# A graph network kernel: taking edges behind sixteen tiles, and loading and turning weights behind the first tiles

## The chip, the cores and the metric

One core of a Trainium2 chip runs the whole program. The metric is the device time of one execution in microseconds, as the median of several runs.

## The reference

Two layers of a graph network on x of 50000 x 256, with one edge list of 75000 edges (12500 random pairs both ways and one loop per node), sorted by target:

```python
h = relu(layernorm(x))
x = x + gcn(h)                # first layer
h = relu(layernorm(x))
x = x + attention(h, src, dst)  # second layer
# gcn: t = h @ w1.T + b1; t = relu(batchnorm(t)); t = (t @ w2.T + b2) @ w_gcn.T
#      degrees by target, norm = dinv[src] * dinv[dst], segment_sum of t[src] * norm
# attention: q, k, v of 8 heads; softmax over the edges of a row; sum of v; @ Wo + bo
```

The batch norm needs the mean and variance of `h @ w1.T + b1` over all rows, so the first matmul must be finished for all rows before the second one starts.

## The kernel before

The program is a row of stages, each a block in which the engines run side by side and meet through semaphores. The change is in the first two.

The rows of x come in 98 tiles of 512 (128 partitions with 4 rows each). **The first stage** (the block that begins at L463, 0 to 607 us) does this for tile t: SP loads x (L499); DVE takes row statistics (L215, four instructions, and L219); ACT takes the root (`a_std`, L648); DVE forms reciprocal and shift (L226, L228); ACT writes the normalised rows `a_hn` (L652, four instructions); PE turns them into `a_turn_ps` (L680); ACT copies that to `a_ht` (L642); PE multiplies by the turned w1 into `a_h_ps`, called `h1_ps` in the code (L702); ACT copies it to `h` with the bias (L634) and stores it (L627); DVE takes its statistics for the batch norm (L1024). Each engine's program is a sequence of steps, and a step holds work of several tiles, in a fixed order: in step s ACT stores tile s-5, copies out `h` of s-4, copies `a_ht` of s-2 and then does root and `a_hn` of tile s; PE turns tile s-1 and multiplies tile s-3; DVE does statistics, one-hots and scale of tile s, then the batch norm statistics of tile s-5, then what is written beside tile s. x, `a_hn`, `a_ht` and `h` have two buffers each, `h1_ps` has one.

Beside the tiles the stage prepares the edges. At tile 1 DVE packs an edge into a word (`pack_words`, L780), at tile 3 it closes the words (`close_words`, L800) and then takes the edges that are no loops out of the 588 columns (`take_all`, L843): a take is a MAX8 on each half of the words and a MATCH_REPLACE8 on each, and moves 16 columns into `found`. The number of takes is read from the data. Tiles 4 to 15 carry twelve steps of class work on the 240 columns found (`beside_tile`, L975, counted from `plan.class_tile` = 4). From `plan.hist_pair` = 8 on, that is tiles 16 to 95, six columns per pair of tiles are counted: DVE makes two one-hots a column (L758, L759), PE multiplies them into `hist_ps` (L672), and POOL scatters the column's words into `dst_slots` (L591), three per tile, each group waiting for `a_hn` of a tile and each scatter for the one three before it. `over_pairs` writes the head of the tiles out and runs the others in a hardware loop.

Ahead of its steps ACT issues seven weight loads (L606 to L610), waits for PE to turn w1 and w_gcn (L731) and copies both (L614), waits for PE's product of w2 and w_gcn and of b2 and w_gcn (L736, L739) and copies these (L616, L617), and issues eight loads of Wo (L621). PE does its part of this ahead of its steps as well, through `turn_ps`.

**The second stage** (the block at L1134, 607 to about 1160 us) closes the batch norm (L1287 on), loads `h` again (L1149), applies the norm (`hb`, L1198), multiplies by the mixed weight (`mix_ps`, L1231), adds the bias (L1310) and stores two scaled copies (L1192, L1161); beside it edges are sorted by source in bodies of six tiles, and the projection weights of the second layer are prepared (`find_peak`, L1321, and `split_weights`, L1326). SP first loads `h` of tiles 0 and 1, stores and loads the small tables (L1168, L1169), then loads the projection weights (L1171 to L1173), and then runs its steps, in which it loads h1 of tile s and stores `agg_table` of tile s-4.

Of the kernel before, what the change touches and what calls it, by code (L numbers as in the profile page):

```python
# [34 lines left out]
P = 128  # L35
D = 256
# [23 lines left out]
class Plan:  # L60


    def __init__(self, n, e):
# [167 lines left out]
def build(nc, x, src, dst, w1, b1, gamma, beta, w2, b2, w_gcn, b_gcn,  # L231
# [20 lines left out]
    with ExitStack() as ctx:  # L252
# [92 lines left out]
        with ExitStack() as part:  # L345
# [117 lines left out]
            with ExitStack() as inner, nc.Block() as block:  # L463
# [23 lines left out]
                def _(sp):  # L487
                    def step(at):
# [11 lines left out]
                        if isinstance(tile, int) and tile == 1:  # L500
                            load_edges()

# [16 lines left out]
                    sp.wait_ge(edges_loaded, 16 * plan.edge_loads)  # L519

# [77 lines left out]
                def _(act):  # L598
# [13 lines left out]
                    for b, w in enumerate((w1_t, wg_t)):  # L612
                        act.wait_ge(weights_turned, b + 1)
                        nc.scalar.activation(w[:, :, :].rearrange("p a b -> p (a b)"), turn_ps[0][:, b * TILE:(b + 1) * TILE], ACT.Copy).then_inc(weights_copied, 1)  # L614
                    act.wait_ge(mixed, 1)
                    nc.scalar.activation(w_mix[:, :, :].rearrange("p a b -> p (a b)"), turn_ps[1][:, 0:TILE], ACT.Copy).then_inc(weights_copied, 1)  # L616
                    nc.scalar.activation(b_mix[:, :], turn_ps[1][:, TILE:TILE + D], ACT.Copy).then_inc(weights_copied, 1)  # L617
                    rows_of_head = wo.rearrange("(d h) n -> h d n", h=H)
                    for h in range(H):
                        kc, first = divmod(h * DH, P)  # L620
                        act.dma_start(w_out[first:first + DH, kc, :], rows_of_head[h]).then_inc(out_loaded, 16)  # L621

                    def step(at):
# [20 lines left out]
                        if at(0) is not None:  # L644
# [9 lines left out]
                            last.then_inc(hn_ready[u], 1)  # L654

                    over_tiles(act, plan, 5, step)
                    act.wait_ge(out_loaded, 16 * H)
# [4 lines left out]
                def _(pe):  # L662
                    def step(at, k, s):
                        if s == plan.degree_step:
                            count_all()
                        if at(1) is not None:
# [15 lines left out]
                            last.then_inc(turned[u], 1)  # L682
                        if s == plan.class_tile + 6:
                            pe.wait_ge(class_ready, 1)
# [40 lines left out]
                    pe.wait_ge(weights_loaded, 16 * 7)  # L725
                    pe.wait_ge(const_ready, const_of_ident)
                    for b, w in enumerate((w1_n, wg_n)):
                        for kc in range(KC):
                            for oc in range(KC):
                                at = b * TILE + kc * D + oc * P  # L730
                                last = nc.tensor.transpose(turn_ps[0][:, at:at + P], w[:, oc, kc * P:(kc + 1) * P], ident[:, :])  # L731
                        last.then_inc(weights_turned, 1)
                    pe.wait_ge(weights_copied, 2)
                    for kc in range(KC):
                        for jc in range(KC):
                            nc.tensor.matmul(turn_ps[1][:, kc * D:(kc + 1) * D], w2_n[:, jc, kc * P:(kc + 1) * P],  # L736
                                             wg_t[:, jc, :], start=jc == 0, stop=jc == KC - 1)
                    for jc in range(KC):
                        last = nc.tensor.matmul(turn_ps[1][:, TILE:TILE + D], b2_c[:, jc:jc + 1].to_broadcast([P, P]), wg_t[:, jc, :],  # L739
                                                start=jc == 0, stop=jc == KC - 1)  # L740
                    last.then_inc(mixed, 1)
                    pe.wait_ge(weights_copied, 4)
                    over_pairs(pe, plan, 3, step, (hist_loop,))

                @block.vector
                def _(dve):
# [53 lines left out]
                    def close_words():  # L800
# [21 lines left out]
                        link(v.tensor_scalar(rounds_f[:, 3:4], rounds_f[:, 2:3], -float(plan.takes_beside - 1), 1.0, ALU.add, ALU.max))  # L822
# [20 lines left out]
                    def take_all():  # L843
# [4 lines left out]
                        hold(dve, replaced, more * 2 + (2 * plan.takes_beside))  # L848
# [126 lines left out]
                    def beside_tile(tile):  # L975
# [29 lines left out]
                    def step(at, k, s):  # L1005
# [27 lines left out]
                    over_pairs(dve, plan, 5, step, (hist_loop,))  # L1033
# [100 lines left out]
            with ExitStack() as inner, nc.Block() as block:  # L1134
# [12 lines left out]
                def _(sp):  # L1147
                    def load_h1(i, u):
# [1444 lines left out]
```

## Time and profile before

| | us |
|---|---|
| median of 3 runs | 3427.66 (3424.08 to 3429.75) |
| profiled execution | 3436.49 |
| its span, first to last instruction | 3434.7 |

| engine | busy us | share |
|---|---|---|
| PE | 3104.5 | 90% |
| DVE | 2809.3 | 82% |
| ACT | 2502.0 | 73% |
| POOL | 1953.0 | 57% |

The span and the windows are of the one profiled execution. A busy time is the union of an engine's instructions; register work, waits and the issuing of DMAs are not counted. "L215" is line 215 of the kernel. A wait in square brackets is the time that the engine sat idle before an instruction, and what ended it. SPq, ACTq and POOLq are the queues in which an engine issues DMAs. `PEclk` is the granted clock of TensorE as a share of 2.4 GHz; 0.50 is 1.2 GHz.

### The profile page before, as it was taken

To read this page: it belongs to the slowest core of one execution; us is meant where nothing else is said; L and a number is where in the kernel's file an instruction comes from. 1 tells how busy PE (TensorE), PEld (TensorE's weight loads), DVE (VectorE), ACT (ScalarE), POOL (GpSimd) and SP (SyncE) were. 2 spreads that over 40 slices of the span, in tenths; PEclk is the share of its full clock that TensorE was granted. 3 is DMA by queue.
4 is the path that set the end of the run, shared out by engine and by line. 5 is a ranking of instruction groups with operands and counts; after the bars stand their busy time and mean duration, and the time that the engine had idled before them with its cause. 6 is when DMAs were issued, how large, how long until landed. Compare 5 with 4: busy or idle time off the path is not lost. (4 is left out here: it accounts for less than half of the span.)

```text
span 3434.7 us, 80752 instructions
## 1 busy us (share of the span) xinstructions
PE 3104.5 (90%) x20244; PEld 2498.7 (73%) x20244; DVE 2809.3 (82%) x7375; ACT 2502.0 (73%) x7074; POOL 1953.0 (57%) x1668
## 2 busy tenths in 40 slices
PE   2899999799998489999999999994999999999999
PEld 1455554577775278787888878883899999999998
DVE  6888887787886478888888888884888888888887
ACT  2688888699896567676777777762777777777776
POOL 1055554155554377777777777763555555555553
PEclk6899999999999699999999999996999999999999
DMA  2455555688886578888878888865677777777774
GB/s 76 147 204 203 203 202 182 233 300 309 301 306 234 206 271 297 305 296 293 304 293 303 296 305 293 302 257 182 230 249 258 258 254 250 254 254 257 254 248 157
DMA packets 335634, 861.27 MB, mean 251 GB/s; under 512 B 98484, under 2 KB 152923, under 8 KB 323019
## 3 DMA queue, kind: packets, MB, share of 16 engines
q1 hardware_dynamic: 238794, 677.69, 55.3%
q0 software_dynamic: 66256, 78.94, 7.7%
q10 hardware_dynamic: 30512, 103.83, 7.6%
q8 instruction: 27, 0.44, 0.1%
q14 instruction: 45, 0.36, 0.0%
HBM read 521.95 MB, written 416.52 MB: 273 GB/s over the span
## 5 line engine op out<-in xcount | busy, mean ns | idle before, releaser
L1848 PE MATMUL c_qkv_ps<-w_qkv_hi,c_ht_hi 128*128 128x256 f16 x2352 | 642.3, 273 | 0.0
L1848 PE MATMUL c_qkv_ps<-w_qkv_lo,c_ht_hi 128*128 128x256 f16 x2352 | 642.3, 273 | 0.0
L1848 PE MATMUL c_qkv_ps<-w_qkv_hi,c_ht_lo 128*128 128x256 f16 x2352 | 642.3, 273 | 0.0
L2281 ACT ACTIVATE e_mine<-e_mine,e_attention 128x32 f32<-128x32 f32 x2352 | 518.7, 308 | 42.3 <-issue 26.1
L2228 POOL DMA_INDIRECT e_kv<-kv_table,e_near x392 | 401.5, 1024 | 113.4 <-issue 102.7
L1718 POOL DMA_INDIRECT c_got<-y_table,c_near x392 | 395.1, 1008 | 108.7 <-issue 87.9
L591 POOL DMA_INDIRECT dst_slots<-dst_word,dst_goal x240 | 241.3, 1005 | 304.3 <-ACT a_hn L652 235.9
L2317 PE MATMUL e_out_ps<-w_out,e_mean_t 128*128 128x256 f32 x1568 | 392.8, 380 | 0.0
L2220 POOL TENSOR_TENSOR e_kv<-e_kv,e_part_of 128x1024 f32<-128x1024 f32 x98 | 187.0, 1908 | 350.8 <-DVE e_part_of L2550 350.8
L702 PE MATMUL a_h_ps<-a_ht,w_t 128*128 128x512 f32 x784 | 368.9, 614 | 17.8 <-ACT h L634 13.9
L1482 POOL DMA_INDIRECT src_slots<-staged_word,staged_goal x240 | 235.2, 980 | 254.5 <-DVE sort_lane_hot L1371 119.2
L1231 PE MATMUL mix_ps<-w_mix,hb 128*128 128x256 f32 x1568 | 358.0, 382 | 12.7 <-ACT hb L1198 9.8
L1231 PEld LDWEIGHTS mix_ps<-w_mix,hb 128*128 128x128 f32 x1568 | 297.2, 191 | 59.0 <-ACT hb L1198 12.6
L1711 POOL TENSOR_TENSOR c_x<-c_agg,c_x 128x1024 f32<-128x1024 f32 x98 | 231.4, 2361 | 161.3 <-ACT c_agg L1765 151.9
L2317 PEld LDWEIGHTS e_out_ps<-w_out,e_mean_t 128*128 128x128 f32 x1568 | 267.4, 191 | 44.0
L1835 PE MATMUL c_sum_ps<-c_got,c_sum_hot 128*128 128x256 f32 x784 | 217.2, 400 | 87.3 <-DVE c_agg L1957 58.5
L702 PEld LDWEIGHTS a_h_ps<-a_ht,w_t 128*128 128x128 f32 x784 | 144.8, 195 | 184.2 <-issue 184.1
L1776 ACT ACTIVATE c_hn<-c_x,c_shift,c_rstd 128x256 f32<-128x256 f32 x392 | 203.5, 590 | 95.7 <-DVE c_shift L1978 94.8
L1703 POOL TENSOR_TENSOR c_qk<-c_q,c_kv 128x1024 f32<-128x1024 f32 x98 | 232.0, 2367 | 34.9 <-DVE c_kv L1942 32.6
L1848 PEld LDWEIGHTS c_qkv_ps<-w_qkv_lo,c_ht_hi 128*128 128x128 f16 x2352 | 230.5, 98 | 27.1
L1848 PEld LDWEIGHTS c_qkv_ps<-w_qkv_hi,c_ht_lo 128*128 128x128 f16 x2352 | 230.5, 98 | 27.1
L2273 ACT ACTIVATE e_mean_t<-e_mean_ps 128x512 f32<-128x512 f32 x196 | 114.9, 586 | 184.9 <-PE e_mean_ps L2331 163.8
(433 smaller groups left out, 7781.8 us busy)
## 6 DMA issues: line engine op xcount, KB each, us to landing
kv_table<-c_kv SPq DMA_DIRECT2D x98, 1024.0 KB
h_table<-h ACTq DMA_DIRECT2D x98, 512.0 KB
h<-h_table SPq DMA_DIRECT2D x98, 512.0 KB
y_table<-y_out ACTq DMA_DIRECT2D x98, 512.0 KB
agg_table<-agg_out SPq DMA_DIRECT2D x98, 512.0 KB
c_agg<-agg_table SPq DMA_DIRECT2D x98, 512.0 KB
x_table<-c_x SPq DMA_DIRECT2D x98, 512.0 KB
q_table<-c_q SPq DMA_DIRECT2D x98, 512.0 KB
```

The source lines that it names most:

```text
L591: nc.gpsimd.indirect_dma_start(out=dst_slots, out_offset=bass.IndirectOffsetOnAxis(ap=dst_goal[:, k:k + 1], axis=0), in_=dst_word[:, k:k + ...
L702: last = nc.tensor.matmul(h1_ps[:, oc * TILE:(oc + 1) * TILE], w1_t[:, kc, oc * P:(oc + 1) * P], ht[u][:, kc, :], start=kc == 0, stop=kc = ...
L1231: last = nc.tensor.matmul(mix_ps[u][:, j * D:(j + 1) * D], hb[u][:, kc, j * P:(j + 1) * P], w_mix[:, kc, :], start=kc == 0, stop=kc == KC - 1)
L1482: nc.gpsimd.indirect_dma_start(out=src_slots, out_offset=bass.IndirectOffsetOnAxis(ap=staged_goal[h][:, k:k + 1], axis=0), in_=staged_word ...
L1703: nc.gpsimd.tensor_tensor(qk[u][:, :, :], qb[w][:, :, :], kv[w][:, :, 0, :], ALU.mult).then_inc(qk_ready, 1)
L1711: nc.gpsimd.tensor_tensor(x1[u][:, :, :], agg[w][:, :, :], xb[w][:, :, :], ALU.add).then_inc(x1_ready, 1)
L1718: nc.gpsimd.indirect_dma_start(out=got[w][:, j, :], out_offset=None, in_=y_table, in_offset=bass.IndirectOffsetOnAxis(ap=near[w][:, j:j + ...
L1835: last = nc.tensor.matmul(sum_ps[:, j * D:(j + 1) * D], sum_hot[w][:, row, :], got[w][:, row, :], start=True, stop=True)
L1848: last = nc.tensor.matmul(qkv_ps[n][:, j * D:(j + 1) * D], h[u][:, kc, j * P:(j + 1) * P], wt[:, kc, n * D:(n + 1) * D], start=m == 0, sto ...
L2228: nc.gpsimd.indirect_dma_start(out=kv[w][:, j, :], out_offset=None, in_=kv_table, in_offset=bass.IndirectOffsetOnAxis(ap=near[w][:, j:j + ...
L2281: last = nc.scalar.activation(of_head, of_head, ACT.Copy, scale=attention[u][:, j, h, 0:1])
L2317: last = nc.tensor.matmul(out_ps[:, j, :], mean_t[u][:, kc, row * P:(row + 1) * P], w_out[:, kc, :], start=False, stop=kc == KC - 1)
```

## The change

Three parts. First, the weights are turned and mixed within the first steps (PE: turning at step 2, the mix at step 3, its bias at step 5, in `h1_ps` and `hist_ps`; ACT: the copies behind tiles 1, 4 and 5), and the Wo loads go to SP, behind the edge loads. Second, the takes: one behind each of tiles 4 to 19, and a loop of at least one more at tile 20 (`take_rest`). `class_tile` becomes 20 and `hist_pair` 16; the 240 columns are then counted in 30 pairs instead of 40 (`hist_most` 8 instead of 6), so four columns and four scatters a tile. The head, seven pairs with takes, the class tiles and 27 counting pairs alternate between written-out turns and two hardware loops. Third, SP's loads of the projection weights come behind h1 of tile 5, and `find_peak` behind tile 5 instead of tile 3.

```diff
-        self.takes_beside = -(-self.wide // TAKEN)
-        self.most_extra = max(1, self.most_takes - self.takes_beside + 1)
-        self.class_tile = 4
+        self.take_pair = 2
+        self.take_pairs = 8
+        self.takes_beside = 2 * self.take_pairs
+        self.most_extra = max(1, self.most_takes - self.takes_beside)
+        self.class_tile = 2 * (self.take_pair + self.take_pairs)
...
+                take_loop = (3, plan.take_pair + plan.take_pairs)
...
-                    return k is not None or i - plan.hist_pair in hist_pairs
+                    return k == 1 or (k is None and i - plan.hist_pair in hist_pairs)
...  SP, first stage, behind load_edges() at tile 1
+                            for h in range(H):
+                                kc, first = divmod(h * DH, P)
+                                sp.dma_start(w_out[first:first + DH, kc, :], rows_of_head[h]).then_inc(out_loaded, 16)
...  ACT, end of step
+                            if isinstance(i, int) and i * 2 + u == 1:
+                                copy_weights()
+                            if isinstance(i, int) and i * 2 + u == 4:
+                                copy_mix()
+                            if isinstance(i, int) and i * 2 + u == 5:
+                                copy_mix_bias()
...  PE, between turning tile s-1 and multiplying tile s-3
+                        if s == 2:
+                            turn_weights()
+                        if s == 3:
+                            mix_weights()
+                        if s == 5:
+                            mix_bias()
...
-                    over_pairs(pe, plan, 3, step, (hist_loop,))
+                    over_pairs(pe, plan, 3, step, (take_loop, hist_loop))
...  DVE
-                        link(v.tensor_scalar(rounds_f[:, 3:4], rounds_f[:, 2:3], -float(plan.takes_beside - 1), 1.0, ALU.add, ALU.max))
+                        link(v.tensor_scalar(rounds_f[:, 3:4], rounds_f[:, 2:3], -float(plan.takes_beside), 1.0, ALU.add, ALU.max))
...
-                        with dve.Fori(0, more + (plan.takes_beside - 1)) as n:
-                            take(n)
+                        with dve.Fori(0, more) as n:
+                            take(n + plan.takes_beside)
...
                             close_words()
-                            take_all()
+                        elif 0 <= tile - 2 * plan.take_pair < plan.takes_beside:
+                            take(tile - 2 * plan.take_pair)
                         elif at == 0:
+                            take_rest()
                             decode_words()
...
-                            if k is None:
+                            if k == 0:
+                                take(i * 2 + (u - 2 * plan.take_pair))
+                            elif k is None:
                                 beside_tile(i * 2 + u)
...  SP, second stage, in step; the same loads are gone from before over_tiles
+                            if isinstance(i, int) and i * 2 + u == 5:
+                                load_qkv()
...
-                            if isinstance(b, int) and b == 0 and t == 3:
+                            if isinstance(b, int) and b == 0 and t == 5:
                                 find_peak()
```

## Rows read from the trace of the kernel before

**Rows 1.** The page, busy time, share of the span and instructions.

```profile
PE 3104.5 (90%) x20244; PEld 2498.7 (73%) x20244; DVE 2809.3 (82%) x7375; ACT 2502.0 (73%) x7074; POOL 1953.0 (57%) x1668
```

**Rows 2.** Windows: busy us and count by engine, then clock, DMA share, GB/s.

```profile
60.00:80.00 20.00, 0.00 (x0) 0.00 (x0) 19.45 (x89) 0.26 (x1) 0.00 (x0) 0.50 0.00 0
...
120.00:140.00 20.00, 16.53 (x65) 8.63 (x64) 13.37 (x52) 14.01 (x28) 0.00 (x0) 1.00 0.43 157
...
200.00:560.00 360.00, 349.80 (x1317) 185.00 (x1316) 316.67 (x1251) 312.07 (x626) 208.83 (x209) 1.00 0.57 203
```

**Rows 3.** Timeline of the head: start us, duration us, engine, line, operation.

```profile
15.24 3.78 PE L736 MATMUL a_turn_ps<-wg_t,w_n 128*128 128x256 f32 x8 [1.67 <-ACT wg_t L614]
...
24.43 1.28 ACT L648 ACT_TABLE_LOAD   x1 [2.88 <-issue]
...
26.06 0.18 DVE L226 RECIPROCAL a_rstd<-a_std 128x4 f32<-128x4 f32 x1 [19.53 <-ACT a_std L648]
...
36.01 1.40 DVE L215 BATCH_NORM_STATS2 a_stats<-a_x 128x6 f32<-128x256 f32 x4
```

**Rows 4.** The takes: timeline of DVE, and line 836 by itself.

```profile
49.85 0.17 DVE L826 CAST rounds<-rounds_f 128x4 int32<-128x4 f32 x1
...
77.88 1.41 DVE L215 BATCH_NORM_STATS2 a_stats<-a_x 128x6 f32<-128x256 f32 x4 [0.22 <-DVE words L841]
...
L836 DVE MAX8 edge_best<-words x30: 442/452/467, 51.4 to 76.2; 128x8 f32<-128x294 f32 x30
```

**Rows 5.** Timeline of DVE in the class tiles and behind them.

```profile
116.89 0.18 DVE L226 RECIPROCAL a_rstd<-a_std 128x4 f32<-128x4 f32 x1 [0.36 <-ACT a_std L648]
...
123.63 0.18 DVE L226 RECIPROCAL a_rstd<-a_std 128x4 f32<-128x4 f32 x1 [3.44 <-ACT a_std L648]
...
161.84 1.41 DVE L215 BATCH_NORM_STATS2 a_stats<-a_x 128x6 f32<-128x256 f32 x4 [0.21 <-DVE uneven_cols L940]
...
576.57 1.39 DVE L215 BATCH_NORM_STATS2 a_stats<-a_x 128x6 f32<-128x256 f32 x4
```

**Rows 6.** Timeline of ACT at a tile without one-hots.

```profile
582.61 1.27 ACT L634 ACTIVATE h<-a_h_ps,bn_in 128x512 f32<-128x512 f32 x2 [0.17 <-PE a_h_ps L702]
```

**Rows 7.** Timeline of PE: a product among class tiles, columns and product in the loop.

```profile
115.38 5.61 PE L702 MATMUL a_h_ps<-a_ht,w_t 128*128 128x512 f32 x8
...
302.38 0.66 PE L672 MATMUL hist_ps<-hot_hi,hot_lo 128*128 128x392 f16 x3
...
303.99 3.67 PE L702 MATMUL a_h_ps<-a_ht,w_t 128*128 128x512 f32 x8
```

**Rows 8.** Timeline of DVE: one tile of the loop with three columns.

```profile
305.03 0.18 DVE L226 RECIPROCAL a_rstd<-a_std 128x4 f32<-128x4 f32 x1 [0.21 <-issue]
...
308.30 0.38 DVE L219 BATCH_NORM_AGGREGATE a_moments<-a_stats 128x2 f32<-128x6 f32 x4
308.70 0.32 DVE L758 TENSOR_SCALAR hot_hi<-lane,dst_key 128x392 f16<-128x392 f16 x1
...
310.29 0.18 DVE L226 RECIPROCAL a_rstd<-a_std 128x4 f32<-128x4 f32 x1 [0.32 <-ACT a_std L648]
```

**Rows 9.** Timeline of POOL: one of six scatters in a row.

```profile
479.54 0.97 POOL L591 DMA_INDIRECT dst_slots<-dst_word,dst_goal  x1 [0.30 <-issue]
```

**Rows 10.** The second stage: timeline of its start, one window behind it.

```profile
620.00 0.43 SPq L1171 DMA_DIRECT2D w_qkv<-in_L_gnn_Wq  x1
...
630.97 2.93 ACT L1198 ACTIVATE hb<-h,bn_shift,bn_scale 128x512 f32<-128x512 f32 x4 [11.96 <-DMA h<-h_table]
...
632.54 3.72 PE L1231 MATMUL mix_ps<-w_mix,hb 128*128 128x256 f32 x16 [2.39 <-ACT hb L1198]
...
637.50 0.44 SPq L1149 DMA_DIRECT2D h<-h_table  x1
...
641.99 1.52 ACT L1198 ACTIVATE hb<-h,bn_shift,bn_scale 128x512 f32<-128x512 f32 x2 [0.30 <-DMA h<-h_table]
...
700.00:1060.00 360.00, 340.72 (x1672) 262.82 (x1671) 289.74 (x1073) 326.45 (x696) 189.15 (x235) 1.00 0.87 305
```

More of the change, by code:

```diff
@@ L611, in _, with copy_weights, copy_mix, copy_mix_bias @@
                     act.wait_ge(const_ready, const_of_ident)
[L612 to L621, printed above, removed]
+                    def copy_weights():
+                        for b, w in enumerate((w1_t, wg_t)):
+                            act.wait_ge(weights_turned, b + 1)
+                            nc.scalar.activation(w[:, :, :].rearrange("p a b -> p (a b)"), h1_ps[:, b * TILE:(b + 1) * TILE], ACT.Copy).then_inc(weights_copied, 1)
+                    def copy_mix():
+                        act.wait_ge(mixed, 1)
+                        nc.scalar.activation(w_mix[:, :, :].rearrange("p a b -> p (a b)"), hist_ps[:, 0:TILE], ACT.Copy).then_inc(weights_copied, 1)
+                    def copy_mix_bias():
+                        act.wait_ge(mixed, 2)
+                        nc.scalar.activation(b_mix[:, :], hist_ps[:, 0:D], ACT.Copy).then_inc(weights_copied, 1)
                     def step(at):
@@ L723, in count_all @@
                         last.then_inc(all_used, 1)
-                    pe.wait_ge(weights_loaded, 16 * 7)
-                    pe.wait_ge(const_ready, const_of_ident)
[L727 to L740, printed above, removed]
@@ L741, in _, with turn_weights @@
-                    last.then_inc(mixed, 1)
-                    pe.wait_ge(weights_copied, 4)
-                    over_pairs(pe, plan, 3, step, (hist_loop,))
+                    def turn_weights():
+                        pe.wait_ge(weights_loaded, 16 * 7)
+                        for b, w in enumerate((w1_n, wg_n)):
+                            for kc in range(KC):
+                                for oc in range(KC):
+                                    at = b * TILE + kc * D + oc * P
+                                    last = nc.tensor.transpose(h1_ps[:, at:at + P], w[:, oc, kc * P:(kc + 1) * P], ident[:, :])
+                            last.then_inc(weights_turned, 1)
+                        pe.wait_ge(weights_copied, 2)
@@ new lines, in mix_weights, with mix_bias @@
+                    def mix_weights():
+                        for kc in range(KC):
+                            for jc in range(KC):
+                                last = nc.tensor.matmul(hist_ps[:, kc * D:(kc + 1) * D], w2_n[:, jc, kc * P:(kc + 1) * P],
+                                                        wg_t[:, jc, :], start=jc == 0, stop=jc == KC - 1)
+                        last.then_inc(mixed, 1)
+                    def mix_bias():
+                        pe.wait_ge(weights_copied, 3)
+                        for jc in range(KC):
+                            last = nc.tensor.matmul(hist_ps[:, 0:D], b2_c[:, jc:jc + 1].to_broadcast([P, P]), wg_t[:, jc, :],
+                                                    start=jc == 0, stop=jc == KC - 1)
+                        last.then_inc(mixed, 1)
@@ L841, in take, with take_rest @@
                             v.match_replace(out=here, in_to_replace=best[h][:, :], in_values=here, imm_value=NONE).then_inc(replaced, 1)
-                    def take_all():
+                    def take_rest():
                         dve.wait_ge(const_ready, const_all)
                         more = dve.value_load(rounds[0:1, 3:4], min_val=0, max_val=plan.most_extra - 1) + 1
-                        with dve.Fori(0, more + (plan.takes_beside - 1)) as n:
-                            take(n)
-                        hold(dve, replaced, more * 2 + (2 * plan.takes_beside))
+                        with dve.Fori(0, more) as n:
+                            take(n + plan.takes_beside)
+                        hold(dve, replaced, more * 2 + (2 * plan.takes_beside + 2))
                     def decode_words():
@@ L1031, in step @@
                             count_all()
-                    over_pairs(dve, plan, 5, step, (hist_loop,))
+                    over_pairs(dve, plan, 5, step, (take_loop, hist_loop))
                     for u in two:
@@ L1147, in _, with load_qkv @@
                 def _(sp):
+                    def load_qkv():
+                        for i, (w, b) in enumerate(((wq, bq), (wk, bk), (wv, bv))):
+                            sp.dma_start(w_qkv[:, :, i * D:(i + 1) * D], w.rearrange("(c p) n -> p c n", p=P)).then_inc(qkv_loaded, 16)
+                            sp.dma_start(b_raw[:, i * D:(i + 1) * D], b.partition_broadcast(P)).then_inc(qkv_loaded, 16)
+                        sp.dma_start(b_out_n[:, :], bo.partition_broadcast(P)).then_inc(qkv_loaded, 16)
                     def load_h1(i, u):
```

8 lines of the change are left out of this document (3 added, 5 removed).

## The prediction

> **What bounds the kernel now.** The page comes first: PE is busy for 90% of the span [rows 1], so what can be won lies in the stretches where it is not. The windows of that stage show three states: 60 to 80 us with no matmul at all, 120 to 140 us with PE at 16.5 of 20, and 200 to 560 us with 349.8 of 360 [rows 2]. So a whole run of time is lost in the first 160 us, and later the stage runs close to PE's limit. I date everything by VectorE's (DVE's) first instruction of a tile, the row statistics of L215: with tN for tile N, t2 is 36.01, t4 is 77.88, t16 is 161.84 and t96 is 576.57 [rows 3 to 5]. There are four of them in a tile.
>
> Three things hold the head. ScalarE (ACT) copies weights and issues eight loads of the output weight before its first `a_std`, so DVE waits 19.53 us for tile 0 [rows 3]. Behind tile 3 DVE does 30 MAX8 and their replacements in one piece, and PE runs dry [rows 2, 4]. Tiles 4 to 15 carry the class work on DVE: 161.84 - 77.88 = 83.96 us for twelve tiles, with DVE itself waiting at some (3.44 us at tile 10) [rows 5].
>
> From t16 on, 80 tiles take (576.57 - 161.84) / 80 = 5.184 us each. Three limits nearly coincide there. (a) One PSUM buffer: `h1_ps` is filled in 3.67 us [rows 7], then ACT copies it out in 1.27, 0.17 after PE's end [rows 6]: 5.11 us, which I take as the beat of a tile without one-hots, 5.12. (b) PE's own work: 360 / 5.184 = 69.4 tiles with 349.8 busy are 5.04 us each, 0.66 of it three columns, or 0.22 each [rows 2, 7]. (c) DVE: from one reciprocal to the next 310.29 - 305.03 = 5.26, of which 0.32 is waiting, so 4.94; its one-hots run from 308.70 to 309.97, 0.42 a column; all else is 3.67 [rows 8].
>
> **The change part by part**, as DVE's tile dates. The sum is made against the profiled execution, 3436.49 us (span 3434.7 and 1.8 around it), which is 8.8 us above the median of 3427.66; I apply the difference to the median.
>
> *Weights behind the first tiles.* DVE's statistics of tile 0 are done at 26.06 - 19.53 = 6.53. From ACT's table load to the reciprocal it is 26.06 - 24.43 = 1.63 [rows 3], so the reciprocal starts near 8.2 instead of 26.06: -17.9 us. Seven loads stay ahead of it on ACT's queue. The eight loads of `w_out` move to SP's queue, behind the edge loads; SP's next job, x of tile 2, waits for tile 0's `a_hn`, which ends near 10.7 (after the reciprocal as now), and at some 0.4 us an issue the fourteen loads are out by then. Tile 1 then starts 2.7 us later as now, packing starts near 11.2 and t2 is about 18.1 (36.01 - 17.9). The packing needs the edges. The load of x of tile 2 has from 10.7 to 18.1 to land; a load of as many bytes takes 4.5 (637.50 to 641.99) [rows 10].
> The weight work moves into PE's and ACT's queues at tiles 1 to 5. Behind PE's matmuls for the mix at step 3 (3.78 us [rows 3]) and the fewer for its bias at step 5 (half as many) stand the products of tiles 0 and 2, behind these `h` on ACT, and behind `h` the `a_std` of tiles 4 to 6, for which DVE waits. For tile 4: tile 2's `a_hn` ends near 22.8, turning it at half clock 24.8, the mix 28.6, product 0 near 33.2 (4.5, part of it warm), `h` and `a_ht` of ACT 35.7; DVE has had its statistics since 32.1 + 1.8 = 33.9, and waits 2 us. Tile 5 waits as long, tile 6 about 1.
>
> *The lump goes.* 30 MAX8 are 15 takes; from 51.4 to 77.66 (77.88 less its wait) they last 1.75 us each, 26.3 in all, and 27.9 with the value load ahead (tile 3's other work ends at 49.85 + 0.17, the next statistics start at 77.88) [rows 4]. So t4 becomes 77.88 - 17.9 - 27.9 = 32.1.
>
> *Sixteen tiles with a take.* DVE's tile without one-hots has 3.67 less the 0.40 from aggregate to one-hots, plus the aggregate and the then open wait for `a_std`, 0.38 + 0.36 = 0.74 [rows 5, 8]: 4.01, plus 1.75: 5.76 us, above the 5.12 of (a), so DVE sets the beat. ACT's round, 312.07 / 69.4 = 4.50 busy [rows 2] and some 0.44 of waiting for the shift, is 4.94 and hides under it. Fourteen such tiles are 80.6; tiles 4 and 5 with the waits above 13.0, and 0.8 more at tile 6: 94.4. t20 = 32.1 + 94.4 = 126.5.
>
> *One extra take and the class tiles.* The loop for the rest takes at least once, so there are 17 takes, 2 more than now; one stands at tile 20 with its value load: 1.39 + 1.75 + 0.3 = 3.4 us. The twelve class tiles are the same work, 84.0, but tile 20 has the `bn_stats` of a tile five back, which tile 4 did not: +1.2. t32 = 126.5 + 88.6 = 215.1.
>
> *Eight columns a pair.* 240 columns in 30 pairs instead of 40. The work is the same, but the beat is another: DVE 4.94 + 0.42 = 5.36, PE 5.04 + 0.22 = 5.26, the buffer 5.12. A low bound is PE's 5.26; a high one has DVE's and PE's extra both in line behind today's beat, 5.184 + 0.42 + 0.22 = 5.82. I take 5.37, since DVE waits 0.32 a tile now and that wait is used up first. 60 tiles are 322.2. POOL's scatters go from three to four a tile; in bunches they come every 1.28 us (0.97 and 0.30 between them) [rows 9], 4 x 1.28 = 5.12 a tile: they just keep up, and where they lag a few tiles nothing waits for them before the end of the stage. Four more tiles at 5.12 lead to t96: 215.1 + 322.2 + 20.5 = 557.8, against 576.57: **-18.8 us**.
>
> *Projection weights behind h1.* Today SP issues seven loads from 620.00 on, ahead of h1 of tile 2; ACT waits 11.96 us for it, until 630.97 [rows 10]. After, that load leaves at 620.0 and lands near 625 (4.5 as above), 6 us earlier. PE was not idle that long: it waits 2.39 at tile 2 [rows 10], and then its queue waits once more on DVE, whose mix waits on ACT's backlog. So 2.4 to 6.0 are to be had; I take 3.5. The 1.25 MB now go out behind tile 5's h1 near 632, into a stretch whose DMA share is 0.87 in the steady state [rows 10]; the next h1 is needed some 10 us later. The peak search, also moved by two tiles, finds its data there. Low bound of the gain: 0, if the burst gives it all back (1.25 MB at 305 GB/s is 4.1 us).
>
> Sum: -18.8 - 3.5 = -22.3, so 3427.7 - 22.3 = **3405.4 us**. A difference of 0.2% (6.9 us) is about what a measurement can tell from none.
>
> **The rivals.**
> *R1, the class tiles gain too* (chance 0.12). The wait of 3.44 us at tile 10 [rows 5] stands behind a product of 5.61 us [rows 7], a PE that runs slow; with one like it at another tile some 7 us could go if sixteen running tiles keep PE's clock up, and the pair loop could be PE-bound at 5.26 (-6.6). That gives 3392. For it: no matmul ran in 60 to 80 us, where the clock was 0.50 [rows 2]. Against: that product stands 35 us behind the idle stretch, among class tiles that stay as long as they are.
> *R2, the clock in the take tiles* (0.07). PE idles about 1 us in each tile of 5.76. At 115.38, among class tiles, the product took 5.61 instead of 3.67 [rows 7]. With 5.61 + 1.44 = 7.05 a tile, fourteen tiles cost 18 more: 3423, no change. Against: 120 to 140 us has PE at 16.5 of 20 and the clock at 1.00 [rows 2]. The Trainium skill, "TensorE: Matmul & The Clock Gate", section "A second HAM failure mode: psum-queue depth-cycling", says that frequent short idling between groups of matmuls can make the clock swing; by that rule this rival would come true, and the stretch just named speaks against it.
> *R3, the added column meets the loop in full* (0.10). The three limits are so close that the 0.42 falls on the beat and some of PE's 0.22 as well: 5.6, halfway from 5.37 to the bound of 5.82, gives 60 x 0.23 = +14, 3419.
> *R4, slower* (0.04). In the take loop PE stays at half clock throughout: the product is 7.34 (twice 3.67), the beat 7.34 + 1.44 = 8.78, fourteen tiles cost (8.78 - 5.76) x 14 = 42 more: 3448. It decides from 2.1 us more per take tile on, (22.3 + 6.9) / 14. For it only the slow product of rows 7; against it that PE at half clock would be busy without gaps.
> *R5, the change only moves the takes* (0.03): a wait in the head that I don't see (edges, `w_out` behind them) gives the 17.9 us of the head back: 3423.
>
> **How the numbers follow.** The forecast has 0.64, and the likeliest value is its own, 3405.4. Its working is uncertain by about 6 in the pair loop, 5 in the class tiles, 3 each in head and second stage. The range reaches down to R1 and up to R3, from 3390 to 3420, and leaves out R2, R4, R5 and the tails, some 0.2. Faster by over 0.2%: forecast, R1 and most of R3, 0.86. Within 0.2%: R2, R5, the rest of R3, 0.09. Slower: R4 and what I don't foresee, 0.05.
>
> **What would show it.** Right: the first reciprocal near 8.2 us; no stretch without matmuls after 20 us; 34 MAX8, of which 32 lie between 36 and 125 us; statistics of take tiles every 5.7 to 5.8 us; t32 near 215 and t96 near 558; pairs of one-hot tiles every 10.7 us with DVE without waits before its reciprocal; ACT's wait for tile 2's h1 cut to 6 us. Wrong: a granted clock under 0.9 in 60 to 125 us (R2, R4), a tile of more than 5.5 us with one-hots (R3), an ACT wait on h1 near tile 6 of the second stage that is as long as the one removed.

## The result, and the profile after

| | kernel before | changed kernel |
|---|---|---|
| median of the runs | 3426.73 us (4 runs) | 3580.36 us (4 runs, 3563.99 to 3586.22) |
| profiled execution | 3436.49 us, span 3434.7 | 3581.81 us, span 3580.0 |
| mean granted clock of TensorE | 0.967 | 0.953 |
| ratio | | 1.0438, 95% interval 1.0423 to 1.0453 |

The forecast was 3405.4 us, the range 3390 to 3420: the change came out on the other side, 175 us above it. No rival gave that time or that cause.

The head did what was forecast. The timeline of DVE in the changed kernel:

```profile
7.96 0.18 DVE L228 RECIPROCAL a_rstd<-a_std 128x4 f32<-128x4 f32 x1 [1.70 <-ACT a_std L659]
...
17.97 1.41 DVE L217 BATCH_NORM_STATS2 a_stats<-a_x 128x6 f32<-128x256 f32 x4
...
32.25 1.41 DVE L217 BATCH_NORM_STATS2 a_stats<-a_x 128x6 f32<-128x256 f32 x4 [0.25 <-DVE rounds L856]
...
115.08 0.18 DVE L228 RECIPROCAL a_rstd<-a_std 128x4 f32<-128x4 f32 x1 [0.37 <-ACT a_std L659]
120.88 0.18 DVE L228 RECIPROCAL a_rstd<-a_std 128x4 f32<-128x4 f32 x1 [0.36 <-ACT a_std L659]
...
210.17 1.40 DVE L217 BATCH_NORM_STATS2 a_stats<-a_x 128x6 f32<-128x256 f32 x4 [0.22 <-DVE uneven_cols L970]
```

These answer to [rows 3 to 5]: the first reciprocal at 7.96 (26.06 before), t2 at 17.97, t4 at 32.25, take tiles 5.80 apart, and t32 at 210.17, 4.9 us ahead of the forecast. The loss begins where the scatters begin. Windows of the changed kernel (columns as in [rows 2]) and the page's busy line:

```profile
60.00:80.00 20.00, 16.75 (x60) 8.29 (x58) 17.66 (x72) 15.20 (x31) 0.00 (x0) 1.00 0.50 184
120.00:140.00 20.00, 14.13 (x47) 6.70 (x46) 18.01 (x69) 13.45 (x27) 0.00 (x0) 0.97 0.40 147
200.00:560.00 360.00, 260.46 (x899) 134.32 (x898) 225.11 (x912) 203.51 (x408) 168.97 (x171) 0.84 0.38 132
320.00:340.00 20.00, 6.81 (x23) 3.45 (x22) 7.35 (x32) 5.68 (x12) 7.54 (x8) 0.66 0.23 79
345.00:355.00 10.00, 9.95 (x39) 5.15 (x37) 9.30 (x36) 8.09 (x17) 7.55 (x8) 1.00 0.57 206
```

```profile
PE 3137.8 (88%) x20244; PEld 2505.7 (70%) x20244; DVE 2814.6 (79%) x7391; ACT 2501.7 (70%) x7073; POOL 1952.2 (55%) x1668
```

PE has 260.46 of 360 us where it had 349.80. It isn't slow throughout: from 345 to 355 it is busy 9.95 of 10, from 320 to 340 only 6.81 of 20. t96 starts at 724.64 instead of 557.8. The page's sums nearly hide this [rows 1]: PE's same 20244 matmuls take 33 us more, the other engines' sums differ by 5 us or less, and PE's share falls by two points. The waits from 200 to 560 us (engine, line, what it waited for; sum, times, longest) name the place:

```profile
POOL dst_slots L599 <- ACT a_hn L663: 311.7, 12, 188.7
PEld a_h_ps L725 <- issue: 182.5, 299, 13.4
ACT h L645 <- remote: 94.7, 10, 13.4
PE a_h_ps L725 <- ACT h L645: 88.6, 11, 13.2
...
DVE a_moments L221 <- remote: 18.0, 5, 4.9
```

ACT stands ahead of `h`, and PE behind it, because `h1_ps` is one buffer. "remote" means that the profile found no instruction whose end explains the release. ACT may wait there for the product, for the statistics of `h` two tiles back, or for the store of that `h`. One such wait in the timeline:

```profile
347.10 0.34 ACTq L638 DMA_DIRECT2D h_table<-h  x1
...
350.61 3.67 PE L725 MATMUL a_h_ps<-a_ht,w_t 128*128 128x512 f32 x8
...
353.48 1.39 DVE L217 BATCH_NORM_STATS2 a_stats<-a_x 128x6 f32<-128x256 f32 x4
...
358.89 0.38 DVE L221 BATCH_NORM_AGGREGATE a_moments<-a_stats 128x2 f32<-128x6 f32 x4 [4.02 <-remote]
...
364.35 0.97 POOL L599 DMA_INDIRECT dst_slots<-dst_word,dst_goal  x1 [0.30 <-issue]
367.58 1.27 ACT L645 ACTIVATE h<-a_h_ps,bn_in 128x512 f32<-128x512 f32 x2 [13.13 <-remote]
```

I read this at first as the store of `h`, issued at 347.10 and landing 20 us later; the expectations below were written with that theory, and it is wrong. Two rows speak against it. The aggregate at 358.89 stands behind DVE's own statistics and nothing else, and still it came 4.02 us late. And the DMA view of 360 to 370 us of the same kernel (busy tenths and GB/s in 40 slices) shows no load or store still moving:

```profile
DMA  0000000000000000000000000000000000000000
GB/s 0 0 0 2 0 0 0 0 2 0 0 0 0 2 0 0 0 0 2 1 0 0 0 1 1 0 0 0 0 0 0 0 0 0 0 0 0 0 0 0
DMA packets 160, 0.00 MB, mean 0 GB/s; under 512 B 160, under 2 KB 160, under 8 KB 160
```

The trace's records of semaphore changes settle what ACT waited for. Of that store's 16 landing records three were kept, the last at 349.65, so they prove little. The last matmul of the product, which carries the increment, ended at 354.28 (the profile models the ends of matmuls); the increment is recorded at 367.42, and ACT's own instruction that waits for it, and for nothing else, follows at 367.45. It is not alone: four increments of PE, by matmuls that ended from 350.70 to 355.82, are recorded in a row from 367.27 to 367.58. DVE's statistics ended at 354.87, their increment is recorded at 358.76. So **increments of PE and DVE that others wait for arrive up to 13 us after the work**, while the next scatters go on. Counted over 200 to 760 us, of 222 waits of over 0.15 us that end with a recorded increment, 27 end with one more than 0.8 us late, 178 us of lateness in all (DVE's part of it runs at the same time as ACT's).

The kernels were measured in seven sittings, and these fall into two kinds. In one, A, the kernel before takes 3388 to 3389 us; in the other, B, 3427 to 3437. The two measurements above are of kind B. The results name chips 1, 5, 6 and 7 for A and 15 and 6 for B; that of the first sitting names none. Executions within a sitting agree within 0.7%, so ratios are only made within one. The waits put down to "remote" occur in B alone, in the kernel before too: its gather stage, 1200 to 2200 us, which I hadn't read, has this row, and the same view of before_scatter8_b (described below) in an A sitting has none of its kind there:

```profile
ACT c_ht_hi L1742 <- remote: 48.4, 40, 1.8
...
DVE c_agg L1957 <- remote: 3.1, 13, 0.3
```

The first stage of the kernel before is the same in both: t96 is 576.57 in its own trace and 576.40 in before_scatter8_b. Its 40 us between the kinds lie behind that stage.

### The profile page after: what moved, and what is told of

The parts are those of the page before. It is cut to its first block and busy times, and to the rows that moved or that the text cites. A ratio compares the mean times of both kernels' runs of the same rounds, so it can differ in the third digit from the quotient of the medians.

```text
span 3580.0 us, 80615 instructions
## 1 busy us (share of the span) xinstructions
PE 3137.8 (88%) x20244; PEld 2505.7 (70%) x20244; DVE 2814.6 (79%) x7391; ACT 2501.7 (70%) x7073; POOL 1952.2 (55%) x1668
## 5 line engine op out<-in xcount | busy, mean ns | idle before, releaser
L725 PE MATMUL a_h_ps<-a_ht,w_t 128*128 128x512 f32 x784 | 399.7, 657 | 157.3 <-ACT h L645 147.5
L725 PEld LDWEIGHTS a_h_ps<-a_ht,w_t 128*128 128x128 f32 x784 | 156.5, 210 | 339.6 <-issue 336.1
L645 ACT ACTIVATE h<-a_h_ps,bn_in 128x512 f32<-128x512 f32 x196 | 123.6, 681 | 210.4 <-remote 146.5
```

The lines of the kernel that those rows point to most:

```text
L725: last = nc.tensor.matmul(h1_ps[:, oc * TILE:(oc + 1) * TILE], w1_t[:, kc, oc * P:(oc + 1) * P], ht[u][:, kc, :], start=kc == 0, stop=kc = ...
```

## The experiments

### Scatters out, or fewer (A sitting, kernel before 3388.60 us)

after_no_scatter leaves all scatters out; after_scatter6 issues six a pair and leaves the last 48 out; after_scatter7 issues all 240, seven a pair, from one pair earlier on.

```diff
                     for k in range(WIDTH):
-                        pair, c = divmod(k, per_pair)
-                        pair += plan.hist_pair
+                        pair, c = divmod(k, 7)
+                        pair += plan.hist_pair - 1
...
-                        if c == per_tile:
+                        if c == 4:
...
```

> The changed kernel without the 240 scatters into dst_slots (that part of the edge order is left out; the one-hots and the counting stay). Theory A, the unbroken stream of scatters holds up the stores of h: ACT's 14 waits ahead of h in the pair loop, 142 us, are gone, and the kernel takes about 3580 - 142 - 30 = 3405 to 3430 us. Theory B, four columns a tile overload DVE, PE and ACT with each other: the waits stay, over 3540 us.

> The changed kernel with eight columns a pair, but the scatters at the old pace of six a pair; the last 48 of 240 are left out. Theory A: POOL pauses 2.8 us a pair again, stores land, 3400 to 3420 us. Theory B: over 3540 us. A third theory, that it is the number of software DMA descriptors in the stage and not their pace: about 80% of the loss stays, 3545 us.

> The changed kernel with eight columns and seven scatters a pair, the first of them one pair earlier, all 240 done. POOL needs 7 x 1.28 = 9.0 of 10.7 us and pauses 1.7. Theory A, if any pause of over a microsecond is enough: 3400 to 3415 us, faster than the kernel before. Theory A, if the stream must be looser than that: between 3420 and 3580. Theory B: 3580.

before_scatter8 is the kernel before (six columns) with `divmod(k, 8)` for the scatters, in two groups of four.

> The kernel before, with its six columns a pair, but eight scatters a pair: each group of four waits for the same tiles as in the changed kernel. Nothing else is changed. Theory A: the waits of ACT ahead of h appear here too, 30 pairs of them, 3540 to 3580 us. Theory B: 3427, as before.

Measured: 3358.68, 3358.55, 3361.27 (ratio 0.9924, 0.9907 to 0.9940) and 3385.21 us; all but the third are single executions. None has a "remote" wait ahead of `h`. All three variants of the changed kernel beat the kernel before by 27 to 30 us, which said little about the scatters, since the changed kernel hadn't been measured in such a sitting. That came next.

### The changed kernel again (A sitting, kernel before 3388.98 us)

> The changed kernel itself, unchanged, beside variants of it on one chip. If the loss belongs to the program, the ratio is 1.04 again, with waits of 7 to 13 us ahead of h. If it belongs to the chip or moment of that measurement, this gives the ratio that the tile dates before t32 promise, 0.992 to 0.994.

> The variant with seven scatters a pair a second time, beside the changed kernel itself. Theory A, the unbroken stream of scatters holds up the stores: 0.992, far below the changed kernel. If the loss was not of the program: the two are equal.

before_cols8 sets `self.hist_most = 8` in the kernel before: eight columns and eight scatters a pair, and nothing else.

> The kernel before with eight columns and eight scatters a pair from pair 8 on, 30 pairs instead of 40, nothing else changed. Theory A with the four-column beat as its condition: ratio 1.03 to 1.045, with the waits ahead of h. Without any stall only the beat changes: 60 tiles at about 5.3 and 20 at 5.12 instead of 80 at 5.18, +5 us, ratio 1.001.

> The kernel before with six columns and eight scatters a pair again. On the other occasion it took the same time as the kernel before; if the stream of scatters alone can start the waits, and the occasion decides, it has them here, over 3480 us where the kernel before has 3427.

Measured: after_again 3363.75 us, **0.9923 (0.9907 to 0.9940)**; after_scatter7_b 3359.52, 0.9913 (0.9896 to 0.9929); before_cols8 3396.44, 1.0023 (1.0013 to 1.0033); before_scatter8_b 3388.62 (one execution). The very kernel that lost 4.4% gains 0.8%. Its waits from 200 to 560 us:

```profile
POOL dst_slots L599 <- ACT a_hn L663: 202.1, 7, 189.9
...
POOL dst_slots L599 <- DMA dst_slots<-dst_word,dst_goal: 35.1, 51, 1.6
...
PE a_h_ps L725 <- ACT h L645: 2.9, 6, 0.6
ACT h L645 <- PE a_h_ps L725: 2.7, 11, 0.3
```

No "remote", and of 273 waits from 200 to 760 us, counted as above, none ends with an increment over 0.8 us late. PE is busy 351.07 of the 360 us. POOL now waits 51 times for a scatter to land; in the changed kernel's first trace it was 5 times. That gave the next theory: that such pauses let other traffic through.

### Four scatters in flight, seven a pair, the third part alone (B sitting, kernel before 3433.05 us)

```diff
+                    put, base = dst_put + [zeroed], (0, 0, 0, 64)
...
-                        if k >= ahead:
-                            pool.wait_ge(dst_put[k % ahead], 16 * (k // ahead))
+                        if k >= 4:
+                            pool.wait_ge(put[k % 4], base[k % 4] + 16 * (k // 4))
...
```

> The changed kernel a third time, as the yardstick of this occasion. Either 1.044 with the kernel before near 3427 and waits ahead of h, or 0.992 with the kernel before near 3389 and none. If the kernel before decides, the two go together; if the loss comes by the program's luck on any chip, they need not.

> Seven scatters a pair, beside the changed kernel. Theory A (the unbroken stream of scatters starves the stores, where scatters land soon): 0.992 on any occasion. Theory C (the loss has another cause than the scatters): as the changed kernel, 1.04 where that has it.

> The changed kernel with four scatters in flight instead of three. On the occasion with 0.992 POOL waited 51 times, 35 us in all, for a scatter to land, and these waits were the only gaps in its stream; with four in flight they go. Theory A, in that the gaps let the stores through: waits ahead of h appear, over 1.01. If the gaps mean nothing: the same time as the changed kernel.

part_qkv is the kernel before with `load_qkv()` behind `load_h1` of tile 5 and the peak search two tiles later.

> The kernel before with the third part alone: the projection weights behind h1 of tile 5, the peak search two tiles later. By the prediction -3.5 us, between 0 and -6: ratio 0.999. If the burst collides in the second stage: 1.000 or above.

Measured: after_third 3579.16 us, 1.0416 (1.0393 to 1.0439), with 149.3 us of "remote" ahead of `h`; after_scatter7_c 3487.81, 1.0154 (1.0124 to 1.0184), with 65.5 us; after_ahead4 3591.88, 1.0447 (1.0410 to 1.0483), with 149.5 us; part_qkv 3434.67, 1.0008 (0.9999 to 1.0018). So the loss goes with the sitting and repeats there; these waits rise with the density of scatters, from none at six a pair (the kernel before and part_qkv have no such wait in this stage) over 65 at seven to 149 at eight. Seven a pair fits neither expectation written for it, 0.992 or 1.04. The changed kernel with six a pair wasn't measured in a B sitting. Fewer pauses for landings don't add to it, where they are few already; the theory of the pauses gained nothing.

The third part: ACT's timeline in part_qkv.

```profile
623.92 1.52 ACT L1202 ACTIVATE hb<-h,bn_shift,bn_scale 128x512 f32<-128x512 f32 x2 [4.65 <-PE mix_ps L1235]
...
639.85 1.52 ACT L1202 ACTIVATE hb<-h,bn_shift,bn_scale 128x512 f32<-128x512 f32 x2 [1.05 <-DMA h<-h_table]
...
648.25 1.52 ACT L1202 ACTIVATE hb<-h,bn_shift,bn_scale 128x512 f32<-128x512 f32 x2 [3.69 <-DMA h<-h_table]
```

`hb` of tile 2 starts at 623.92 instead of 630.97 [rows 10], but with the burst of weights in the queue, at 634.6 to 639.6, `h` is late at the tiles behind it, by 1.05 and 3.69. At tile 6, 648.25 against 647.18 in the kernel before, nothing is left of the 7 us. What PE's own backlog had to do with it wasn't separated.

### GpSimd busy, or small transfers from another queue; the head alone (A sitting, kernel before 3388.62 us)

```diff
-                        nc.gpsimd.indirect_dma_start(out=dst_slots, ...)
+                        pool.wait_ge(filled, k)
+                        nc.gpsimd.memset(filler[:, :], 0.0).then_inc(filled, 1)
```

```diff
+                        if not isinstance(tile, int):
+                            for c in range(per_tile):
+                                sp.dma_start(probe[bass.ds((tile * per_tile + c) * 32, 32), :], ident[0:32, c:c + 1]).then_inc(probed, 16)
```

> The kernel before with eight counting columns and eight scatters a pair and nothing else of the change. On the two chips on which the kernel before takes 3389 us this was measured at 1.002 of it. Where the kernel before takes about 3430 us: T (what the changed kernel loses there is the denser stream of scatters alone, and it shows as late semaphore increments of PE's product and of DVE's statistics in the pair loop): 30 pairs at the density of the changed kernel, so the same waits of ACT ahead of h, put down to "remote", 120 to 150 us, and a time 1.03 to 1.045 of the kernel before. Rival V (it needs the changed kernel's head or take tiles as well): under 10 us of such waits and 1.002.

> The changed kernel with each of the 240 scatters replaced by a memset of about the same length on GpSimd; the scatters are left out. It separates GpSimd being busy from what its scatters put on the DMA queues and semaphores. T (traffic of the scatters holds the increments): no waits of ACT ahead of h put down to "remote", and a time under that of the kernel before by the changed kernel's own gain, 0.985 to 0.993 of it, on any chip. Rival U (GpSimd issuing without a pause is enough): the waits stay at 140 us on the chip where the changed kernel had them, 1.04.

> The changed kernel without GpSimd's scatters (left out), and with four small stores a tile (32 x 4 B, 16 increments each) issued by SyncE in tiles 2 to 95 in their place: as many transfers and increments a tile as the changed kernel's scatters, from another queue. T1 (the increments that every transfer sends are what crowds the semaphores): late increments of PE and DVE here too, waits of ACT ahead of h of 50 us or more where the changed kernel has them, in the earlier tiles too, 1.01 to 1.05. T2 (it is the way in which GpSimd's indirect transfers are written and rung): none, 0.985 to 0.995. Where the kernel before takes 3389 us both expect no waits.

part_head is the changed kernel with the takes in one lump, `class_tile` 4, six scatters a pair and the projection weights where they were.

> The first part alone: first tiles ahead of the weights, with the takes in one lump, six scatters a pair and the projection weights as in the kernel before. By the prediction's steps: 17.9 us less, 0.9948 of the kernel before. T: it keeps six scatters a pair, so it gains this on every chip, 0.993 to 0.997, also where the whole change loses 4%. Rival: if the head's gain is taken back by the late increments of the later stages where the kernel before takes about 3430 us, 0.998 to 1.002.

The sitting was of kind A, so the first three could not meet the late increments and had none. before_cols8_b: 3397.33 us, 1.0024 (1.0014 to 1.0035), as on the one earlier occasion (its expectation speaks of two chips). The two substitutes for the scatters, one execution each, cost far more than the scatters, each by a mechanism of its own, and so say nothing on the question they were made for. after_pool_fill: 3492.24 us. Its lines of DVE from 340 to 540 us, and below them those of after_again, for line, operation, count, then busy time and mean ns:

```profile
L785 DVE TENSOR_SCALAR hot_hi<-lane,dst_key 128x392 f16<-128x392 f16 x108 | 84.8, 785 | 0.2
...
L217 DVE BATCH_NORM_STATS2 a_stats<-a_x 128x6 f32<-128x256 f32 x106 | 36.8, 409 | 0.0
...
L228 DVE RECIPROCAL a_rstd<-a_std 128x4 f32<-128x4 f32 x26 | 16.4, 632 | 0.0
```

```profile
L217 DVE BATCH_NORM_STATS2 a_stats<-a_x 128x6 f32<-128x256 f32 x149 | 51.8, 410 | 0.0
L788 DVE TENSOR_SCALAR hot_hi<-lane,dst_key 128x392 f16<-128x392 f16 x144 | 49.5, 344 | 0.3
...
L228 DVE RECIPROCAL a_rstd<-a_std 128x4 f32<-128x4 f32 x38 | 6.3, 167 | 3.1 <-ACT a_std L659 3.1
```

A memset of 1.18 us on GpSimd makes some of DVE's operations wait: the one-hot takes 785 ns for 344 and the reciprocal 632 for 167, the row statistics 409 as ever. The Trainium skill, "SBUF — State Buffer", section "SBUF: two separate sides", says that the two engines share one pair of ports under an exclusive lock that DVE needs only in some modes; that only some kinds of DVE instruction are longer here agrees with it, and the scatters, which last 0.97 us each, didn't do this. after_sp_stores: 3549.93 us. In its waits from 200 to 560 us the load of x comes late:

```profile
DVE a_stats L217 <- DMA a_x<-in_x: 108.5, 35, 7.5
...
ACT h L652 <- DMA h_table<-h: 20.5, 9, 5.3
```

With four stores of 32 x 4 B a tile in SP's queue, the large loads behind them come late; the scatters of the same count do nothing like it in after_again.

part_head: 3372.21 us, **0.9949 (0.9932 to 0.9965)**. By the step's 17.9 us it should be 0.9947.

### The denser scatters alone (B sitting, kernel before 3437.39 us)

> The kernel before with its six counting columns and eight scatters a pair. On the chips on which the kernel before takes 3389 us this was level with it (3385 and 3389 us). Where the kernel before takes about 3430 us: T (the denser stream of scatters alone makes PE's and DVE's increments late): waits of ACT ahead of h put down to "remote", 60 to 150 us in the 30 pairs that scatter, and 1.015 to 1.045 of the kernel before. Rival V (it takes the rest of the change too: the shorter tile, the eight columns, the head): under 10 us of such waits, 0.998 to 1.002.

Measured: 3627.70 us, **1.0555 (1.0537 to 1.0573)**. It is the kernel before with nothing changed but the number of scatters a pair, six to eight. The waits from 200 to 560 us:

```profile
POOL dst_slots L591 <- ACT a_hn L652: 140.8, 12, 15.9
...
ACT h L634 <- remote: 119.4, 10, 13.7
PE a_h_ps L702 <- ACT h L634: 102.9, 19, 13.6
```

Every late increment of the stage that a wait ends on, 14 of them, is that of the product. From 150 to 760 us ACT waits 167.0 us in this way, a little over the 150 expected, and the ratio is over the 1.045 expected. It loses more than the changed kernel does, 190 against 146 us in after_third, which has the change's own gain in it (25 us in A). So the density of the scatters is enough; head, take tiles, eight columns and projection weights aren't needed for it.

### The head alone, once more (A sitting, kernel before 3387.68 us)

> The first part alone again, with six scatters a pair. Where the kernel before takes about 3430 us: T (only the density of the scatters makes the increments late there) gives no waits of ACT ahead of h put down to "remote" and 0.993 to 0.997, as on the chip on which it measured 0.9949; the rival (the head's gain is taken back there) 0.998 to 1.002. Where the kernel before takes 3389 us both expect 0.995 again.

Measured: 3369.54 us, 0.9948 (0.9934 to 0.9961), 18.1 us. The sitting was again of kind A. That the head alone gains in a B sitting is likely, since it keeps six scatters a pair, but it wasn't measured there. The result names chip 6, as does that of before_scatter8_c, nine minutes earlier and of kind B; whether it is the same device in the same machine isn't known.

## Why the prediction was wrong, point by point

The dates of the row statistics, in us:

| | t2 | t4 | t20 | t32 | t96 |
|---|---|---|---|---|---|
| forecast | 18.1 | 32.1 | 126.5 | 215.1 | 557.8 |
| changed kernel, A (after_again) | 18.14 | 32.42 | 124.52 | 211.55 | 550.17 |
| changed kernel, B (first trace) | 17.97 | 32.25 | 124.36 | 210.17 | 724.64 |

ACT's waits ahead of `h` and DVE's ahead of its aggregate in the first trace, from 200 to 760 us:

```profile
ACT h L645 <- remote: 146.5, 15, 13.4
...
ACT h L645 <- PE a_h_ps L725: 54.0, 54, 3.9
...
DVE a_moments L221 <- remote: 32.9, 10, 4.9
```

- **The step that failed** is in "Eight columns a pair": "they just keep up, and where they lag a few tiles nothing waits for them before the end of the stage". The scatters were costed as time on POOL's own queue, 4 x 1.28 = 5.12 us a tile, and there it holds: they come every 1.28 us in both kinds of sitting. What they do to others was costed at nothing. In a B sitting the increments of the product come up to 13 us late with them, and 147 to 150 us of ACT's time ahead of `h` go there. In the first trace ACT idles 204 us ahead of `h` from 200 to 760 us: 146.5 for the late increments and 54.0 for the product itself, for which it waits 12.5 up to the end of the stage in A. PE runs part of that time at the lower clock, 0.85 on average from 200 to 760 us and 0.66 from 320 to 340 us, where it had stood idle. DVE's waits for its own statistics, 32.9 us, all lie inside ACT's and add nothing. Of the 175 us, 167 stand at t96; 7 come from measuring the sum against the kernel before's profiled execution, which was 8.8 us over its median, where the changed kernel's was 1.5 over. before_scatter8_c shows that denser scatters alone turn the sign.
- The forecast had a warning within reach. The kernel before's own trace is of kind B, and its gather stage, where POOL issues gathers in bunches 1.3 us apart (1008 ns each and 0.30 between them), has 40 waits ended by nothing that the profile knows. I read only the stages that the change touches. No wait of the stage itself, at six scatters a pair, showed it; but records of semaphore changes were missing there already, 4.6 a us from 300 to 340 us against 18.4 in part_head (A, also six a pair).
- *Head*: right. The reciprocal at 7.96 for 8.2; part_head measured 16.4 and 18.1 us for 17.9.
- *Lump and take tiles*: right in kind, and 2 us too dear by t20. DVE's waits at tiles 4 to 6 came smaller, 0.36, 1.45 and 0.36 us in A where about 2, 2 and 1 were forecast.
- *Class tiles*: 88.6 forecast, 85.8 to 87.1 in the traces of the changed kernel and its variants with scatters, with no difference between the kinds.
- *Pair loop*: without late increments t32 to t96 takes 338.6 us, forecast 342.7: 60 tiles at 5.31 for 5.37, and four at 5.02 for 5.12. Eight columns alone should cost 60 x (5.37 - 5.184) less 20 x (5.184 - 5.12), 10 us; before_cols8 measured 7.5 and 8.7 us.
- *Projection weights*: -3.5 forecast, +1.6 measured (1.0008, interval 0.9999 to 1.0018). The low bound, no gain, came true, and by the dates of `hb` for the reason named there: the burst gives it back.
- *The rivals*. R2 and R4 have the clock low in the take tiles: it is 1.00 from 60 to 80 us. The rule cited with R2, from the Trainium skill, "TensorE: Matmul & The Clock Gate", section "A second HAM failure mode: psum-queue depth-cycling", did not come true at 16.75 us of PE in 20. R1 came true in small part: in A the class tiles gained 1.6 of its 7 us and the pair loop 4.1 of its 6.6; with the take tiles' 2.0 that makes 7.6 us by t96. R3 and R5 didn't occur. The rival of the other side, R4, had the right sign and the wrong place.
- In an A sitting the change brings -25.2 us (3363.75 against 3388.98) where the sum said -22.3. So the sum was of the right size for the work it counted, and the sign of the result hung on a thing that it didn't count.

**What stays open**: what holds the increments. What can be said is where they are late: in B sittings only, where POOL's indirect transfers are dense, in this stage and in the gathers. In those sittings records of semaphore changes are missing as well: 37,839 in the trace of the kernel before and 39,486 in that of the changed one, against 59,367 to 59,877 in traces of kind A with all scatters. Most of what the changed kernel lacks, 17,508 of 20,045, are landings of DMAs; its instructions and DMA packets are all there in both kinds. From 120 to 200 us, without scatters, both kinds have 6.4 to 6.6 a us for the changed kernel; from 300 to 340, with scatters, it is 19.6 in A and 3.6 in B.

It is not the increments alone that are held: instructions that only change registers or branch (PE, DVE, ACT and SP) last over 0.5 us 102 times of 12,630 in the changed kernel's first trace, up to 1.40, and several fall into the waits just shown (four of DVE's from 359.55 to 363.02); in after_again the longest of the same 12,630 takes 0.23, and none in any other kind A trace with scatters is over 0.5. Every timed execution here was a recorded one, as each lists its clock and span. So the recording may itself be what backs up, and no run here tells whether an unrecorded execution would be late too. The Trainium skill, "NOTIFIC — Programmer's Manual", section "When the ring fills", says that a full queue of records either drops new ones, overwrites old ones or stalls the producer; the missing records agree with the first, the late increments would be the last, and no run here tells them apart. Missing records alone cost no time there: the kernel before lacks them from 300 to 340 us in B, and its t96 is that of before_scatter8_b in A.

Nor was it tried whether six scatters a pair with sixteen take tiles, which would need room for 48 more scatters elsewhere, wins in both kinds. The version that rests on the firmest ground is part_head: 0.995 in two A sittings, and nothing in it makes the scatters denser.

## What to carry to other kernels

Cost a transfer that is issued more often not only by its issuing engine's time but by what it does to the rest: look in the trace of before for waits that end with nothing the profile names ("remote" here), in every stage and not only in the one changed, and ask what engine streams there. When the same kernel's time depends on the sitting, run the changed kernel and the kernel before again elsewhere before explaining the difference: here the sign depended on it. And a wait's label is an inference: the instruction ahead of which it stands may wait for several semaphores, and only their own records say which came last.

## What the runs showed of the hardware that I had not expected

- In B sittings alone: increments of PE and DVE up to 13 us late, with PE idle and the DMA engines all but idle (0 to 2 GB/s), while GpSimd issued a scatter of 128 words every 1.28 us; no such wait at one scatter in 1.7 us on average (six in 10.4 us), 65 us of them at seven a pair, 149 at eight in the changed kernel and 167 at eight in the kernel before.
- In the same traces, register and branch instructions that take up to 1.4 us (102 of 12,630 over 0.5 in the first trace of the changed kernel), where the median is 0.04; in after_again none over 0.23.
- Small stores from SyncE's queue cost more than the scatters (3549.93 against 3363.75 us, both in A): with four of 32 x 4 B a tile the two hardware queues take 60.6 and 28.4% of the DMA engines' time from 100 to 200 us for 137 GB/s, where after_again, still without scatters there, has 22.7 and 18.7% for 152 GB/s.
- A GpSimd memset of 1.18 us makes DVE's one-hot 2.3 times and its reciprocal 3.8 times as long, and leaves the row statistics as they are.
